# Four narrow transpositions of router logits become one full one, in a mixture-of-experts kernel on one core

## The reference

```python
probs = jax.nn.softmax(xf @ router_w + router_b, axis=-1)
eid = jnp.argmax(probs, axis=-1)
onehot = jax.nn.one_hot(eid, E, dtype=xf.dtype)
rank = (jnp.cumsum(onehot, axis=0)[jnp.arange(N), eid] - 1.0).astype(jnp.int32)
valid = rank < C
...
y_tok = y[eid, pos] * vmask
yov = jax.nn.relu(xf @ ow1 + ob1) @ ow2 + ob2
out = y_tok + yov * (1.0 - vmask)
```

## Time and profile before

| what | value |
|---|---|
| runs of the kernel | 1201.78 us median of 3 (1201.62 to 1203.48) |
| the profiled execution | 1200.27 us, its span 1198.4 us |
| mean granted TensorE clock | 0.985 |
| busy: TensorE, its loads | 1147.7 us, 1027.2 us |
| busy: VectorE, ScalarE, GpSimd | 1005.6 us, 733.2 us, 687.7 us |
| instructions | 24542 |

### The profile page before, as it was taken

How to read it: one execution, slowest core, us unless ns; L and a number is a source line. 1 busy time by engine, 2 the same in 40 slices (tenths; PEclk the granted TensorE clock), 3 DMA queues, 4 the chain that set the end, 5 groups by cost and what they waited for, 6 DMA issues and landing times.

```text
span 1198.4 us, 24542 instructions
## 1 busy us (share of the span) xinstructions
PE 1147.7 (96%) x7657; PEld 1027.2 (86%) x7657; DVE 1005.6 (84%) x2735; ACT 733.2 (61%) x1293; POOL 687.7 (57%) x803
## 2 busy tenths in 40 slices
PE   5489999999999999999999999999999999999994
PEld 4378888898888888888888888889888888899994
DVE  4698888888988898888888888898889987778883
ACT  3256566666666666665656666566656666677883
POOL 4565556665565556566656566565656664414452
PEclk9699999999999999999999999999999999999997
DMA  8211111111111111001001111111111100335530
GB/s 256 88 37 45 54 50 47 42 38 35 35 35 35 35 35 35 23 30 35 30 22 35 35 35 35 35 35 35 35 35 35 35 18 19 101 123 184 167 108 25
DMA packets 59429, 65.10 MB, mean 54 GB/s; under 512 B 7835, under 2 KB 55629, under 8 KB 59268
## 3 DMA queue, kind: packets, MB, share of 16 engines
q1 hardware_dynamic: 52228, 59.36, 15.4%
q0 software_dynamic: 7168, 5.34, 1.5%
HBM read 40.19 MB, written 38.76 MB: 66 GB/s over the span
## 4 chain that ended last, share of the span: by engine, by line
PE 91%; DVE 3%; POOL 3%; ACT 1%; issue 1%; DMA 0%; DVEq 0%; POOLq 0%; ACTq 0%
PE psY L1180 12%; PE psY L1183 11%; PE psY L1182 11%; PE psH L1080 11%; PE psH L1082 11%; PE psH L1081 11%; PE psA L1080 5%; PE psA L1082 5%; PE psA L1081 5%; PE psT L1136 3%; PE psT L1093 2%; PE psT L1142 1%; PE psT L1144 1%; DVE st L709 1%; PE psT L1151 1%
## 5 line engine op out<-in xcount | busy, mean ns | idle before, releaser
L549 ACT ACTIVATE hid<-psH,biasT 128x512 f32<-128x512 f32 (+2 forms) x320 | 206.6, 646 | 265.4 <-PE psH L1082 262.6
L1180 PE MATMUL psY<-W_hi,hid_hi 128*128 128x256 f32 x1200 | 346.5, 289 | 0.5 <-DVE hid_lo L855 0.5
L1183 PE MATMUL psY<-W_hi,hid_lo 128*128 128x256 f32 x1200 | 339.0, 282 | 0.0
L1182 PE MATMUL psY<-W_lo,hid_hi 128*128 128x256 f32 x1200 | 338.8, 282 | 0.0
L372 POOL TENSOR_TENSOR rstd<-veps,mhalf 128x4 f32<-128x4 f32 (+1 forms) x104 | 144.1, 1385 | 192.5 <-DVE nmean L721 192.5
L855 DVE TENSOR_TENSOR hid_lo<-hid,hid_hi 128x512 fp32r<-128x512 f32 (+2 forms) x320 | 205.8, 655 | 46.2 <-ACT hid_hi L553 41.6
L1080 PE MATMUL psH<-xfT_hi,W_hi 128*128 128x512 f32 (+2 forms) x640 | 240.6, 376 | 2.1 <-DVE xfT_lo L799 1.6
L1082 PE MATMUL psH<-xfT_hi,W_lo 128*128 128x512 f32 (+2 forms) x640 | 239.6, 374 | 0.0
L1081 PE MATMUL psH<-xfT_lo,W_hi 128*128 128x512 f32 (+2 forms) x640 | 239.6, 374 | 0.0
L1180 PEld LDWEIGHTS psY<-W_hi,hid_hi 128*128 128x128 f32 x1200 | 226.5, 189 | 10.9 <-DVE hid_lo L855 1.7
L1182 PEld LDWEIGHTS psY<-W_lo,hid_hi 128*128 128x128 f32 x1200 | 226.6, 189 | 6.5
(11 more groups left out here) (115 smaller groups left out, 2114.1 us busy)
## 6 DMA issues: line engine op xcount, KB each, us to landing
xin<-L_attn_x SPq DMA_DIRECT2D x32, 512.0 KB, 3.5
stage<-L_ffn_w SPq DMA_DIRECT2D x16, 1024.0 KB, 5.5
out<-outt SPq DMA_DIRECT2D x31, 512.0 KB, 2.9
xbuf<-zrow SPq DMA_DIRECT2D x1, 2590.0 KB, 19.6
xin<-xbuf SPq DMA_DIRECT2D x8, 259.0 KB, 5.3
stage<-L_ffn_ow SPq DMA_DIRECT2D x2, 1024.0 KB, 10.5
xbuf<-x,idx POOLq DMA_INDIRECT x128, 2.2
b_b<-L_ffn_b SPq DMA_DIRECT2D x1, 1024.0 KB, 13.7
```

The lines of the kernel that those rows point to most:

```text
L549: act.activation(hid[j % 2][:, at:n], psH[:, j % 2, at:n], ACT.Relu, bias=bias).then_inc(s_hid, 1)
L1180: pe.matmul(psY_t[:, t, :], hi, w[0][:, j, :], start=(j == 0 and t % 2 == 0), stop=False, skip_group_check=True)
L1182: pe.matmul(psY_t[:, t, :], hi, w[1][:, j, :], start=False, stop=False, skip_group_check=True)
L1183: last = pe.matmul(psY_t[:, t, :], lo_, w[0][:, j, :], start=False, stop=(j == HC - 1), skip_group_check=True)
```

## The change

ScalarE no longer copies the 16 x 512 logits as one piece. It writes each tile of 128 tokens, 16 partitions high, to a group of 32 partitions of its own in `lgT`, which is now 128 x 128: tile t goes to partitions 32t to 32t + 15. The rows between are zero from one memset on VectorE at the start, for which ScalarE waits once, in the first group. TensorE turns the whole of `lgT` in one full transposition against the full identity. Each token then finds its 16 logits of tile t in columns 32t to 32t + 15 of PSUM, and `logits` has a step of 32 between tiles in place of 16.

```diff
+QUAD = P // TG
...
-        lgT = sb("lgT", [2 * E, GT])
+        lgT = sb("lgT", [P, P])
...
-        logits = psT[:, 1, 0:TG * 2 * E].rearrange("p (t e) -> p t e", t=TG)
+        logits = psT[:, 1, 0:P].rearrange("p (t e) -> p t e", t=TG)
...
             def logits_out(g):
                 act.wait_ge(s_lgT, cnt(g, 1, 1))
                 act.wait_ge(s_lg, cnt(g, 1, 0))
-                act.activation(lgT[:], logitsT, ACT.Copy).then_inc(s_lgT_sb, 1)
+                if not live(grp(g[0], g[1], -1), NG):
+                    act.wait_ge(s_lgT_z, 1)
+                for t in range(TG):
+                    last = act.activation(lgT[t * QUAD:t * QUAD + 2 * E, :], logitsT[:, t * P:(t + 1) * P], ACT.Copy)
+                last.then_inc(s_lgT_sb, 1)
...
             dve.memset(warm[:], 0.0).then_inc(s_warm, 1)
+            dve.memset(lgT[:], 0.0).then_inc(s_lgT_z, 1)
...
             def logits_by_token(g):
                 pe.wait_ge(s_lgT_sb, cnt(g, 1, 1))
                 pe.sem_inc(s_held_pe, 1)
-                for t in range(TG):
-                    last = pe.transpose(logits[:, t, :], lgT[:, t * P:(t + 1) * P], ident[0:2 * E, 0:2 * E])
-                last.then_inc(s_lg, 1)
+                pe.transpose(psT[:, 1, 0:P], lgT[:], ident[:]).then_inc(s_lg, 1)
```

## The result

The changed kernel took **1203.33 us** (median of 20 runs, 1202.54 to 1204.9) against 1201.38 us for the kernel before in as many runs; the ratio is 1.0019, 95% interval 1.0013 to 1.0026. By the ratio that is 2.3 us slower: small, but clear of no change. The executions of either kernel fall into two lots some 1.8 us apart, in unequal shares, and the two medians differ by 2.0 us. The forecast was 1193.8. Rival (c), the wait for ScalarE, was priced at 1204.9.

The account below looks back on a forecast made before the run. TensorE was taken to bound the kernel. Gains of 7.5 us in 29 groups, 0.1 in the first two and 0.45 in the last made 8.0, so 1201.78 - 8.0 = 1193.8 us; range 1189.5 to 1199.9.

Parts of the forecast that it names:

- Rival (c): ScalarE's writes to different partitions don't overlap: series 1.16 us, TensorE waits, 0.12 us lost a group, 1204.9 us; chance 0.10.
- What bounds the kernel: TensorE, busy 96% of the span, runs from instruction to instruction, so what leaves its stream leaves the time.
- the section: TensorE's stretch from the last layer-1 load to the projection's first stream; the four transpositions there cost 0.57 us of it.
- The holes are of the shape: TensorE's idle gaps around the narrow transpositions come from switching 128 to 16 partitions and back; the change removes both.
- The length of ScalarE's series: ScalarE's four writes of lgT overlap by 0.10 us and take 0.78 us, 0.21 more than the single copy.
- the turning point: Length of ScalarE's four writes beyond which the changed kernel is slower: 1.04 us, 0.26 for each added write.
- the stretch behind the load: TensorE from the transposition's load at 462.12 to the projection's first stream at 462.34: 0.11 exposed load plus 0.11.
- the estimate of 0.89 us for four: ScalarE's four writes by the Trainium skill's figures; would shrink the gain from 8.0 to about 4.9 us, 1196.9 us.
- The wait and the counting: TensorE waits for ScalarE's last write, counts a semaphore, then loads: 0.16 us taken, between ends 0.04 and 0.16.
- The sum itself: Whole kernel: 0.26 us gained a group in 29 groups, 0.1 in the first two, 0.45 in the last, together 8.0.
- VectorE's side and the memset: VectorE reads as many logits at stride 32, costed at nothing; the memset stands before its 3.32 us first wait.
- The last group: In the last of 32 groups lgT is early, so TensorE doesn't wait for it and gains 0.45 us.

Follow-up runs that it names:

- experiment 1: Changed kernel with the full transposition moved behind the first six matmuls of the projection, 0.7 us later: 1191.27 us, ratio 0.9913.
- experiment 2: Kernel before, with its four narrow transpositions moved behind the first six matmuls of the projection: 1201.95 us, ratio 1.0005.
- experiment 4: Changed kernel with ScalarE writing only the first tile's logits, so the output is wrong: 1190.96 us, ratio 0.9916.
- experiment 3: Kernel before, with ScalarE's one copy split into four 16x128 writes, all to partitions 0 to 15: 1200.13 us, ratio 0.9997.
- experiment 6: Changed kernel without the semaphore count between TensorE's wait and the transposition: 1199.9 us, ratio 0.9989.
- experiment 5: Changed kernel with lgT 128 x 512, all four writes to partitions 0 to 15, only the first block transposed (output incomplete): 1191.59 us, ratio 0.993.

## Why the prediction was wrong, step by step

**What bounds the kernel: right.** What the section lost showed in the time, to within half a microsecond in the account above.

**The holes are of the shape: right.** Experiments 1, 2 and 4 show it: with the full shape, and lgT in time, both are gone. The cost of a full transposition, 0.11 us, was right where the projection surrounds it (experiment 1); at the original place the section of experiment 4 is 0.59 us, 0.04 above the 0.22 + 0.22 + 0.11 of the prediction. The drain that the Trainium skill's TensorEngine Tiling (Array Packing), "Key Properties", speaks of agrees, if 16 rows are a mode of their own: 0.19 us more to the first narrow load than to the full one at the same place (0.32 against 0.13).

**The length of ScalarE's series: wrong, and this is the step that failed.** "Four take 4 x 0.271 - 3 x 0.10 = 0.78 us". The single write was right (0.265), the overlap of 0.10 was not there: 1.08 us. It came from rows in which activations in a row write the same partitions and different columns; the very thing that the change altered, where each write goes, had no row. Rival (c) named the change of partitions as the reason and set the turning point at 1.04 us. Its own sum has a slip: with a series of 1.16 us lgT isn't early in the last group either, and it took 0.45 off for that group all the same. Put into the forecast's working, the measured 1.08 gives 461.18 + 1.08 + 0.16 + 0.11 + 0.11 = 462.64, 0.04 later than the 462.60 before. That this is just the loss in the odd groups is luck in part: the wait cost 0.05 less than 0.16, and the stretch behind the load 0.04 more than 0.22. I gave it 0.10 because "the overlap holds wherever ScalarE has a series", which was true only of series unlike this one. The step carried the whole forecast, for the wait binds and each tenth of a microsecond in the series is a tenth in the section. The estimate from the Trainium skill's ScalarE: Activation LUTs, "What ACT_TABLE_LOAD costs", has the same overlap, 93 ns, in it. The overlap fits experiment 3 (4 x 0.249 less 0.72 leaves 0.09 for each of three), though the estimate of 0.89 us for four lies above the 0.72 there, since a single write takes 0.249 and not 0.29; for the change it gave 0.89 where the trace shows 1.08. Here the measurement decides.

**The wait and the counting: near at the load, incomplete behind it.** The load came 0.11 us after the last write, within the ends of 0.04 and 0.16 and nearer to the one taken. Not foreseen was that a binding wait also exposes what stands behind it: 0.08 of the counting between the two loads (experiment 6), and 0.09 to 0.10 for the register in the even groups, 14 x 0.09 = 1.3 us of the 2.3. The prediction gave the stretch behind the load 0.22 us, and it took 0.26 in odd groups and 0.35 in even ones.

**The sum itself: right in size for the kernel it described.** Experiment 5 has the overlap and gains (1 - 0.993) x 1200.37 = 8.4 us; the sum said 8.0. The gain a group is 0.32 in odd and about 0.22 in even ones, 0.27 in the mean against 0.26. That it is so close is luck in part: the series was 0.06 us shorter than the 0.78 of the sum and the wait 0.05 shorter than 0.16, and what stood behind the load took that back, 0.04 in odd groups and 0.13 in even ones.

**VectorE's side and the memset: right.** The two reads of `logits` take 0.18 and 0.19 us in both kernels, and the memset 0.17 us at 1.1 us of the span. **The last group: right only for an early lgT.** It gained 0.36 us where I had 0.45, because lgT wasn't early; with one write (experiment 4) it gained 0.44.

**Where the gain is kept.** Experiment 1 gets 9.2 us by the medians, 10.4 by the ratio, of the 13.8 that no wait at all would have given by the prediction. From an odd group's transposition to the next it takes 31.21 us, 0.43 less than before. From an even group's it is mostly 0.06 to 0.11 longer than that, since the next wait has appeared: TensorE's loads of the transpositions of tok now wait for GpSimd in 14 places, where it was one before.

```profile
PEld psT L1100 <- POOL tok L385: 8.6, 14, 3.6
```

## What to carry to other kernels

A saving on the bounding engine that is paid for on an engine feeding it is worth only what the feeder's slack allows: work out by how much the feeder may be late, and look for a row of exactly the kind of series that the change makes, down to the partitions and columns that it writes. When two engines meet too closely, first move the meeting: six matmuls put between turned a loss of 2 us into a gain of 9. And behind a wait that binds, even counting up a semaphore or computing a register costs 0.06 to 0.1 us that is invisible while the engine runs ahead.

## What the runs showed that was not expected

- ScalarE's activations of 16x128 follow each other by 0.157 us when they write the same partitions in four blocks of columns, and by 0.272 us, without overlap, when each writes to another group of 32 in the same columns (0.72 against 1.08 us for four, experiments 3 and 5 against the changed kernel). Which of the two differences does it is not shown.
- Transpositions of 16 partitions in the midst of 128-partition matmuls cost TensorE a hole of about 0.1 us ahead and another behind. Four of them cost 0.57 us, while one full transposition, fed in time, costs 0.11.
- A semaphore count on TensorE is free while its wait is already fulfilled (experiment 1), and costs 0.06 us ahead of the load and 0.08 behind it when the wait binds (experiment 6), as it puts the wait into an instruction of its own.
